# A graph network on one core: source parts, runs of products and window adds re-planned over the last forty units

## The reference

```python
coef = w_comp[etype]
msg = sum_b (x[src] @ weight[b]) * coef[:, b] * norm            # 8 bases
x1 = layernorm(x + relu(segment_sum(msg, dst) + bias_param))
neigh = segment_sum(x1[src] + edge_attr, dst)
h = ((1 + eps) * x1 + neigh) @ W1 + b1                          # 256 wide
out = layernorm(x1 + relu(batchnorm(h)) @ W2 + b2)
```

## Time and profile before

| | us |
|---|---|
| median of 3 runs (lowest, highest) | 617.11 (615.18, 617.66) |
| the profiled execution: its own time, its span | 616.46, 614.7 |
| PE busy, DVE busy, POOL busy, ACT busy | 504.3, 458.2, 402.5, 215.1 |

### The profile page before, as it was taken

How to read it: one execution, slowest core, us unless ns; L and a number is a source line. 1 busy time by engine, 2 the same in 40 slices (tenths; PEclk the granted TensorE clock), 3 DMA queues, 4 the chain that set the end, 5 groups by cost and what they waited for, 6 DMA issues and landing times.

```text
span 614.7 us, 12766 instructions
## 1 busy us (share of the span) xinstructions
PE 504.3 (82%) x3965; PEld 424.5 (69%) x3965; DVE 458.2 (75%) x1812; ACT 215.1 (35%) x309; POOL 402.5 (65%) x434
## 2 busy tenths in 40 slices
PE   4669787887887967887968899788989898799894
PEld 3448676676776655875657787677879897678574
DVE  6998999989887687985798788977753655335466
ACT  9904445453433342432433433333300000002373
POOL 6777777777777777777777777777777777500000
PEclk9988999997887997987997999889989999889998
DMA  5423757574655673755766768664665864650003
GB/s 133 121 54 98 264 184 225 171 241 147 215 172 159 206 237 105 249 158 187 226 216 189 250 213 281 218 222 136 241 209 176 275 217 129 215 192 2 2 11 96
DMA packets 98712, 108.18 MB, mean 176 GB/s; under 512 B 10949, under 2 KB 85686, under 8 KB 98642
## 3 DMA queue, kind: packets, MB, share of 16 engines
q1 hardware_dynamic: 79650, 77.81, 38.4%
q0 software_dynamic: 13312, 27.29, 16.0%
q10 hardware_dynamic: 5680, 2.23, 1.4%
HBM read 81.73 MB, written 25.56 MB: 175 GB/s over the span
## 4 chain that ended last, share of the span: by engine, by line
PE 45%; DVE 34%; DMA 10%; issue 5%; DVEq 2%; POOL 2%; ACT 1%; SPq 0%; ACTq 0%; POOLq 0%
PE psum L1190 15%; PE psum L1107 8%; DVE etype_hot L1573 7%; PE psum L1165 7%; DMA gathered_flat<-in_x_dram,src_i 6%; PE psum L1098 6%; DVE etype_hot L1570 5%; DVE sums_flat L1685 5%; PE psum L1131 4%; DVE weighted L1460 3%; DMA sums_flat<-in_x_dram 3%; POOL gathered_flat L808 2%; DVE adj_flat L1432 2%; PE psum L1328 1%; DVE sums_flat L1650 1%
## 5 line engine op out<-in xcount | busy, mean ns | idle before, releaser
L808 POOL DMA_INDIRECT gathered_flat<-in_x_dram,src_i x416 | 400.2, 962 | 129.8 <-issue 87.5
L893 ACT ACTIVATE adj_flat<-psum 128x500 f16<-128x500 f32 (+1 forms) x208 | 127.3, 612 | 245.4 <-PE psum L1131 239.4
L1098 PE MATMUL psum<-hot,attrs 128*128 128x60 f32 (+3 forms) x832 | 155.9, 274 | 2.4 <-DVE weighted L1460 2.4
L1107 PE MATMUL psum<-weighted,gathered_flat 128*128 128x96 f32 (+1 forms) x832 | 138.3, 292 | 20.1 <-DMA gathered_flat<-in_x_dram,src_i 20.0
L1098 PEld LDWEIGHTS psum<-hot,attrs 128*128 128x128 f32 x832 | 144.2, 207 | 11.7 <-issue 9.2
L1685 DVE TENSOR_TENSOR sums_flat<-psum,sums_flat 128x180 f32 x208 | 71.5, 344 | 101.8 <-PE psum L1098 72.1
L1107 PEld LDWEIGHTS psum<-weighted,gathered_flat 128*128 128x128 f32 x832 | 121.3, 205 | 23.2 <-DMA gathered_flat<-in_x_dram,src_i 23.1
L1573 DVE TENSOR_SCALAR etype_hot<-iota_key,key_t 128x300 f16<-128x300 f16 (+1 forms) x416 | 137.1, 332 | 0.0
L1131 PE MATMUL psum<-etype_hot 128*128 128x300 f16 (+1 forms) x416 | 126.9, 330 | 6.4 <-DVE etype_hot L1573 6.3
L1570 DVE TENSOR_SCALAR etype_hot<-iota_key,gathered_flat 128x128 f16<-128x128 f16 x416 | 107.0, 257 | 0.0
L1190 PE MATMUL psum<-sums_flat 128*128 128x264 f16 x594 | 76.5, 286 | 10.8 <-DVE weighted L1460 10.8
(11 more groups left out here) (154 smaller groups left out, 351.1 us busy)
## 6 DMA issues: line engine op xcount, KB each, us to landing
attrs<-in_edge_attr_dram SPq DMA_DIRECT2D x51, 512.0 KB
adjacency<-adj_flat SPq DMA_DIRECT2D x26, 900.0 KB, 6.2
gathered_flat<-in_x_dram,src_i POOLq DMA_INDIRECT x416, 3.6
coef<-adjacency SPq DMA_DIRECT2D x23, 288.0 KB, 5.5
sums_flat<-adjacency SPq DMA_DIRECT2D x9, 576.0 KB, 6.0
sums_flat<-adjacency SPq DMA_DIRECT2D x13, 288.0 KB, 5.5
sums_flat<-adjacency SPq DMA_DIRECT2D x6, 432.0 KB, 5.5
out_dram<-gathered_flat SPq DMA_DIRECT2D x5, 256.0 KB
```

The costliest lines, as they stand in the source:

```text
L808: pool.indirect_dma_start(gathered[:, t % (RING * GROUP), :], None, x[:, :], bass.IndirectOffsetOnAxis(src_i[:, t:t + 1], 0)).then_inc(gat ...
L893: nc.scalar.activation(window, counts, ACT.Copy).then_inc(counts_copied, 1)
L1098: product = nc.tensor.matmul(echoed_row(u, i), attrs[:, s * GROUP + j, :], hot_tiles(s, i)[:, u % GU, :].unsqueeze(1) .to_broadcast([P, EC ...
L1107: nc.tensor.matmul(unit_psum(u)[:, 0:B, STARTS[i]:STARTS[i] + WIDTHS[i]], gathered[:, (u * UNIT + i) % (RING * GROUP), 0:F], weighted_tile ...
```

## The change

- A looped part of one tile (tile 22) is added; the rest, tiles 23 and 24, become one late part of 181 columns in place of 256 and 53. Its 16-bit parts are kept in the buffer of the attributes, which ACT zeroes past the 53 rows (`zero_late_rows`). DVE's `zero_rest_parts` goes.
- Parts that are finished after counting has ended ("tight": the last three) start at once and have their steps closer together.
- After couple 83 a run may follow every unit, in bank 7, 4, 3 or 5 by `u % 4`, so that bank 7's runs stand after the first unit of a group. `LAST_RUN_UNIT` is 203. From couple 84 the plan has 32 runs with 130 tiles; before it had 20 with 108.
- From couple 86 DVE adds the windows of the last couple's runs ahead of the sums of its own.
- Seven blocks are opened by fills (tiles 20 to 22), which a later step closes in the same bank: two fills after units 206 and 207, five while the late part is normalised, then the first 16-bit part of tiles 23 and 24 for all seven (`first_parts`), then the thirteen finals. What is left to fills and finals: 51 tiles, 73 before.
- SP loads four of the blocks for fills and finals two groups before the end, and the other nine once the last gather has landed; before, seven were issued together during the last group. DVE reads all window places of the finals in couples 98 to 102.

```diff
-    PART_TILES = (4, 4, 4, 4, 2, 2, 2)
+    PART_TILES = (4, 4, 4, 4, 2, 2, 2, 1)
...
-    PARTS += ((LATE_AT, CHUNKS * CHUNK - LATE_AT), (CHUNKS * CHUNK, REST))
-    LATE = (LOOPED, LOOPED + 1)
-    assert max(PART_TILES) == CT and all(n % 2 == 0 for n in PART_TILES) and 0 < N - LATE_AT <= 512
+    LATE_TILES = HIGHS - PART_AT[LOOPED]
+    PARTS += ((LATE_AT, N - LATE_AT),)
+    assert max(PART_TILES) == CT and 0 < N - LATE_AT <= 512 and LATE_TILES == 2
     PART_OF = [(k, h - first // P) for h in range(HIGHS) for k, (first, n) in enumerate(PARTS)
...
-    BACK_AT, ROOT_AT, TURN_AT, KEEP_AT = 1, 3, 8, 9
-    RESIDUAL, NORM, SPLIT, OWN = 0, 2, 3, 5
+    ALL_COUNTED = min(w for w in range(COUPLES) if counted(2 * w) == U)
+    TIGHT = [done_unit(k) > 2 * ALL_COUNTED for k in range(LOOPED)]
+    FIRST = [-(-(done_unit(k) + (0 if TIGHT[k] else 2)) // 2) * 2 for k in range(LOOPED)]
+    AGG_AT = [FIRST[k] + (PART_TILES[k] + 1) // 2 * 2 for k in range(LOOPED)]
+    BACK_AT, ROOT_AT = 1, 3
+    TURN_AT = [5 if TIGHT[k] else 8 for k in range(LOOPED)]
+    KEEP_AT = [TURN_AT[k] + 1 for k in range(LOOPED)]
+    RESIDUAL = 0
+    NORM, SPLIT, OWN = ([tight if TIGHT[k] else wide for k in range(LOOPED)] for tight, wide in ((1, 2), (1, 3), (3, 5)))
...
+    def lead(w):
+        return 2 if w > ALL_COUNTED else 3
...
-    def run_bank_of(w):
+    def run_bank_of(u):
+        w = u // 2
+        if w > ALL_COUNTED:
+            return (7, 4, 3, 5)[u % 4]
+        if u % 2 == 0:
+            return None
         if w % 2 == 0:
             return 7
-        if w > ALL_COUNTED:
-            return 3
-        held = any(first - 2 <= 2 * w + 1 <= at + KEEP_AT + 1 for first, at in zip(FIRST, AGG_AT))
+        held = any(first - 2 <= u <= at + keep + 1 for first, at, keep in zip(FIRST, AGG_AT, KEEP_AT))
...
-            ready = sum(2 * w >= at + 2 * SPLIT + 3 for at in AGG_AT)
+        for u in range(LAST_RUN_UNIT + 1):
+            w = u // 2
+            if run_bank_of(u) is None:
+                continue
+            ready = sum(u >= AGG_AT[k] + 2 * SPLIT[k] + (3 if TIGHT[k] else 4) for k in range(LOOPED))
...
-                if 2 * step + 2 + LEAD <= w:
-                    runs.append((w, b, reached[b], reached[b] + parts, place, step))
+                if 2 * step + 2 + lead(w) <= w:
+                    runs.append((u, b, reached[b], reached[b] + parts, place, step))
...
-    TAIL = spaced(FILLED_BLOCKS, [])
-    LOAD_ORDER = TAIL + [b for b in range(BLOCKS) if b not in TAIL]
-    TAIL = spaced(LOAD_ORDER, TAIL)
-    FINALS = [(b, LAST_RUNS[b][1], PART_AT[LOOPED]) for b in TAIL[:FILL_COUNT]]
-    FINALS += [(b, PART_AT[LOOPED] if b in FILLED_BLOCKS else LAST_RUNS[b][1], HIGHS) for b in TAIL[FILL_COUNT:]]
-    assert all(first < last for _, first, last in FINALS) and len(FINALS) == FILL_COUNT + BLOCKS
-    FINAL_BANKS = (7, 3, 4, 6, 5, 1)
+    TAIL = spaced(BY_REST[FILL_COUNT:], spaced(BY_REST[0:FILL_COUNT], []))
+    FILLS = [(b, LAST_RUNS[b][1]) for b in TAIL[0:FILL_COUNT]]
+    LOAD_ORDER = TAIL
+    assert all(first < PART_AT[LOOPED] for _, first in FILLS)
+    FINAL_BANKS = (7, 4, 6, 5, 1, 3, 2, 0)
+    EARLY_LOADS = 4
...
-                    if g == GROUPS - 1:
-                        load_late_rows_of_x()
-                        for b in LOAD_ORDER[0:6] + LOAD_ORDER[12:13]:
+                    if g == GROUPS - 2:
+                        for b in LOAD_ORDER[0:EARLY_LOADS]:
                             load_last(b)
-                for b in LOAD_ORDER[6:12]:
+                load_late_rows_of_x()
+                sp.wait_ge(gather_in[(U - 1) % RU], U // RU * 16 * UNIT)
+                for b in LOAD_ORDER[EARLY_LOADS:]:
                     load_last(b)
...
+            def zero_late_rows():
+
+                act.wait_ge(sums_mm, COUPLES - GU // 2)
+                n = LATE_TILES * P
+                for r, used in ((0, PARTS[LOOPED][1]), (1, (LATE_TILES - 1) * P)):
+                    zeros = nc.scalar.activation(attrs_flat[:, r * n + used:(r + 1) * n],
+                                                 zero_col[:, 0:1].to_broadcast([P, n - used]), ACT.Copy)
+                zeros.then_inc(rest_zeroed, 1)
...
+                def fill_products(n):
+                    b, first = FILLS[n]
+                    pe.wait_ge(last_in[n], 16)
+                    pe.wait_ge(parts_ready, LOOPED)
+                    block_products(wait_for_bank(n), tiles_in(last_buffer(b), first, first, PART_AT[LOOPED]), closes=False)
...
-                    if u % 2 and u // 2 in RUN_AT:
-                        run_products(RUN_AT[u // 2])
+                    if u in RUN_AT:
+                        run_products(RUN_AT[u])
+                    if u >= U - 2:
+                        fill_products(u - (U - 2))
...
+                    b = TAIL[n]
+                    at = LAST_RUNS[b][1]
+                    first = PART_AT[LOOPED] if n < FILL_COUNT else at
+                    if n >= FILL_COUNT:
+                        pe.wait_ge(last_in[n], 16)
+                        bank = wait_for_bank(n)
                     else:
-                        earlier = [m for m in range(NRUNS) if run_bank(m) == bank]
-                        if earlier:
-                            pe.wait_ge(nbr_added, BLOCK * (earlier[-1] + 1))
-                        if bank == 6:
-                            pe.wait_ge(x1_kept, LOOPED)
-                        if bank < 6:
-                            pe.wait_ge(counts_copied, U)
-                    block_products(bank, tiles)
+                        bank = FINAL_BANKS[n]
+                    pe.wait_ge(parts_ready, LOOPED + 1)
+                    block_products(bank, tiles_in(last_buffer(b), at, first, HIGHS), opens=n >= FILL_COUNT,
+                                   parts=(0, 1, 2) if n >= FILL_COUNT else (1, 2))
+
+                def first_parts(n):
+                    b = TAIL[n]
+                    pe.wait_ge(parts_step, 3 * LOOPED + 1)
+                    block_products(FINAL_BANKS[n], tiles_in(last_buffer(b), LAST_RUNS[b][1], PART_AT[LOOPED], HIGHS),
+                                   opens=False, closes=False, parts=(0,))
...
+                turn_back(LOOPED)
+                for n in range(2, FILL_COUNT):
+                    fill_products(n)
+                turn_norm(LOOPED)
                 for n in range(FILL_COUNT):
-                    final_products(n)
-                for k in LATE:
-                    turn_norm(k)
-                for n in range(FILL_COUNT, len(FINALS)):
+                    first_parts(n)
+                for n in range(BLOCKS):
                     final_products(n)
...
-                    if w - 1 in RUN_AT:
-                        firsts = block_bases(RUNS[RUN_AT[w - 1]][1])
+                    if COUPLES - 6 <= w < COUPLES - 1:
+                        b = len(last_bases) // BLOCK
+                        last_bases += block_bases(b, min(3, BLOCKS - b))
+                    runs = [n for n in range(NRUNS) if RUNS[n][0] // 2 == w - 1]
+                    firsts = {n: block_bases(RUNS[n][1]) for n in runs}
+                    for k in range(LOOPED):
+                        if w == AGG_AT[k] // 2 + OWN[k] + 1:
+                            dve.wait_ge(own_added, k + 1)
+                    adds = [(n, j) for n in runs for j in range(BLOCK)]
+                    if w > ALL_COUNTED + 2:
+                        if adds:
+                            dve.wait_ge(added, 2 * w)
+                        for n, j in adds:
+                            add_run(n, j, firsts[n])
+                        adds = []
                     dve.wait_ge(sums_mm, w + 1)
-                    if runs_before(w - 1) > runs_before(w - 2):
-                        dve.wait_ge(nbr_added, BLOCK * runs_before(w - 1))
-                    for k in range(LOOPED):
-                        if w == AGG_AT[k] // 2 + OWN + 1:
-                            dve.wait_ge(own_added, k + 1)
+                    finished = runs_before(w if w > ALL_COUNTED + 2 else w - 1)
+                    if finished:
+                        dve.wait_ge(nbr_added, BLOCK * finished)
...
+                chunk_residual(LOOPED)
+                chunk_norm(LOOPED)
+                chunk_split(LOOPED, 0)
+                chunk_split(LOOPED, 1)
+                dve.wait_ge(nbr_added, BLOCK * NRUNS)
+                chunk_own(LOOPED)
+                dve.wait_ge(own_added, LOOPED + 1)
```

270 lines of the change are left out of this document (121 added, 149 removed).

## The result

On the first chip the changed kernel takes 638.09 us (median of 4 runs, 637.43 to 639.44), the kernel before 617.38 (4 runs, 615.18 to 617.9). The ratio is 1.0355 (95% interval 1.0329 to 1.038), so 20.7 us slower. I had predicted 621.5 (610 to 628): slower is right, the size is not.

The account below looks back on a forecast made before the run. The prediction took PE's waits for DVE, not gathers, as what counts. Waits of 18.2 us plus 4.8 of slow clock made 23.0 against 18.0 before, 5 us slower: 616.46 becomes 621.5, range 610 to 628.

Parts of the forecast that it names:

- units 168, 172, 176 and 180: PE's runs in bank 7 wait there for DVE's select: 3.3, 1.15, 1.3 and 3.4 us.
- 184, 188 and 200: Shorter PE waits for DVE at these units: 0.36 us each at 184 and 188, 0.6 at 200.
- One of the signs: Sign that the forecast is right: PE leaves unit 207 at 553 to 562 us.
- units 197 and 205: PE's wait in `turn_norm` right behind DVE's normalising: 0.4 and 0 to 2.4 us, entered as 0.4 and 0.6.
- unit 198: The one-tile part's bases wait for DVE's sums of unit 197: 4.0 us without loads, 4.6 with.
- after 207: `bases` waits for DVE's last sums, with DVE ending 1.8 to 3.2 us behind PE: entered as 2.1.
- so I expose one or so at each place where DVE is late: About one uncovered register load, 0.52 us on DVE's queue, of two to four at the heads of couples 86 to 102.
- the three long waits: Slow clock behind PE's long waits: 1.6 us of loss, seen after one of 2.27 us, charged as 4.8 in all.
- the collision: SP's loads slow the last gathers; its end is worth 3.0 us only to a PE waiting for gathers, so nothing.
- late loads: The nine loads of counts behind the last gather have over 10 us, so they cost nothing.
- ring and POOL: PE may fall 40 us behind the gathers before POOL stops; it falls 25 behind, so no cost.
- everything exposed: Rival: all register loads uncovered, 22 us of waits and 6.4 of clock, ending at 627 or more; chance 0.08.

Follow-up runs that it names:

- c0: The changed kernel with no edit, on a slower chip: 757.7 us, ratio 1.0043 to the kernel before.
- c1: The changed kernel with the base numbers of the last 13 blocks read in the tail again: 758.5 us, ratio 1.0074 to the kernel before.
- g8: The changed kernel with runs behind odd units alone from unit 168 on (49 runs, not 63): 747.4 us, ratio 0.993 to the kernel before.
- g0: The changed kernel with no edit, on another slower chip than c0: 758.6 us, ratio 1.0078 to the kernel before.
- e8: The same kernel as g8 (runs behind odd units alone), on another slower chip: 753.5 us, ratio 0.9869 to the kernel before.
- b0: The kernel before, unedited, with a trace on a slower chip: 763.2 us, one run.
- g9: g8 plus the 13 blocks' base numbers read in couples 64 to 72 and late runs' base numbers one couple earlier: 746.5 us, ratio 0.9914 to the kernel before.
- e5: The changed kernel with the 13 blocks' base numbers read in couples 64 to 72, ahead of the unit sums: 763.3 us, ratio 1.0012 to the kernel before.

## Why the prediction was wrong in size

**Right.** The direction, and the work: 975 products in both. PE waits 3.17, 1.20, 1.33 and 3.88 us at units 168, 172, 176 and 180 (predicted 3.3, 1.15, 1.3, 3.4); twice 0.44 and 0.74 for 184, 188 and 200 (0.7 and 0.6 together); no wait for gathers; 40.5 us of dense layers. From the bases at 576.00 to the last product at 595.1 it is 19.1 us (tail 18.9), with a wait of 0.5 ahead of it and not 2.1. One of the signs was missed: unit 207 was left at 574.5, not at 553 to 562.

**First failed step: units 197 and 205, "0.4 and 0 to 2.4", entered as 0.4 and 0.6.** They were 2.06 + 1.19 and 4.10, 7.35 in place of 1.0. In part this was given back at unit 198 (3.26 for 4.6) and after 207. The reason is the sentence "so I expose one or so at each place where DVE is late": ahead of unit 205 there stand, from 556.6 on, two groups of three reads, one of three blocks and two of one in each, 2.5 us a group. In the trace nothing covers them: DVE stands idle for 2.58 us ahead of the window add at 565.59, while PE waits for it. The reads of three blocks I had not priced apart at all. Without them the waits for the normalising fell from 6.4 us (c0) to 3.4 (c1); the rest went only with fewer runs (g8). A read of one block was priced right (0.52 us, measured 0.51), so the error lay in the cover and in the long reads. The Trainium skill gives about 200 ns for each register that a `TENSOR_LOAD` reads, also in bulk (Runtime: NRT & Kernel Launch, section "Instruction fetch mechanics"). The trace agrees for these reads, whose values lie apart in the buffer: 1.40 less 0.51 is 0.22 us for each of the four further registers. It does not agree for the four values of a group's own read (line 1699), which lie side by side: they take 0.35 us together (minimum, median and longest of a read in ns, then when):

```profile
L1699 DVEq TENSOR_LOAD <-base_row x52: 339/349/1567, 48.3 to 569.8; - x52
L1675 DVEq TENSOR_LOAD <-base_row x68: 507/519/2495, 154.0 to 571.3; - x68
```

Both medians are also under the floor of some 600 ns that the prediction cites from the Trainium skill (DMA: Bandwidth & Descriptors, section "Latency and other measured facts"); the measurement decides. I had also not seen that the run behind `turn_norm` at 197 waits for a split that DVE does behind the normalising (1.19). Idle time came to 22.9 where I had 18.2.

**Second failed step: the clock, "I charge that to the three long waits, 4.8".** It cost about 11 us. The wait that I took for the price was one of 2.27 us, followed by 1.6 us of loss. Behind 3.17 us that held (3.2 us at 1.2 GHz, 2.96 of them busy, so 1.5 lost); behind the others it was more: 6.6 us at 1.2 GHz behind 3.88, 10.1 behind 2.06, 1.19 and 3.26, 6.7 behind 4.10. The kernel before held a dearer case than the one I took, which I had read only as an average (0.82):

```profile
536.40:543.20 6.80, 6.37 (x30) 4.98 (x30) 1.28 (x4) 0.00 (x0) 0.00 (x0) 0.50 0.56 207
```

It stands behind a stop of 1.89 us and cost about 3. In c0, g0, e8 and b0 too, slow stretches follow most stops of 1.8 us or more (12 of 14, the other two lie in a stretch that was slow already) and few of the shorter ones. But stops do not explain all: in g9, whose longest stop is 1.6 us, PE was at 1.2 GHz for 18 of the 136 us. Over the stretch, 22.9 us of idle time came with about 11 of slow clock. This is read from traces; no run changed the clock alone, and what sets it is not shown.

**Third: the 5.1 us before unit 168,** which the prediction took to be equal. 1.7 are slow clock behind the stop of 1.94 us at 444.16: from the start of these 24 products to the next unit it is 4.37 us. In the kernel before it is 2.70, and the same stop there is 1.48 us long, so another 0.5 is the longer stop. The other 3.0 were there at unit 164, where both plans issue the same on PE. On chip D the kernels reach unit 168 at 568.1 and 567.1. Why it was 5 on the first chip stays open.

The three together, 4.7 of idle time, 6.2 of clock and 5.1, are 16.0; the profiled execution took 637.43, 15.9 above my number.

**The costs put at nothing:** the collision, late loads, ring and POOL cost nothing (no wait for a gather or a load stands among PE's waits, and POOL idles 130.1 us, before 129.8). The early reads' cover, which I did not ask for, was what failed. The rival *everything exposed* (627, "or more where a wait that I did not see joins", chance 0.08) was nearest. That its 22 us of waits come so close to 22.9 is luck: it exposed loads at other places, and units 198 and the end came in 2.9 below my own terms. Its clock, 6.4, was too low too.

**How far it is shown.** That DVE's late work makes the stops is shown by runs on the other chips, where the same stops stand in the same places and shrink or go with the edits. How much each edit would take off the 20.7 us of the first chip is not shown.

## What to carry to other kernels

Moving TensorE work forward pays only as long as the engine that must fold its results in can follow. Here 12 more late runs brought 24 more window adds and 12 more register reads to a VectorE for which PE already waited 6.6 us. Two ways out gave about 1% each against the kernel before: fewer late runs, although 36 products went back to the tail, or all runs with the reads moved ahead, each with the run that waits for the select one unit later. Ask of each read what it waits behind, and take its price from a read of the same length and layout. A read hoisted from one busy place to another gained nothing in time (c1 against c0); read where VectorE waited for PE, it cost nothing in the stretch or in the tail (e5).

## What the runs showed of the hardware

- A register read on DVE took 0.51 us for two registers and 1.40 for six, whose values lie apart in the buffer, and 0.35 for four that lie side by side.
- On four other chips the kernel before took 22 to 23% longer. POOL started a gather every 1.57 us in b0 (399.3 and 253.5 us over 416) and every 1.27 on the first chip, and DVE and PE paused too with nothing shown that they waited for. My expectations say that the engines stood still together; I saw that in one place of one trace only, and there PE's products went on. Over the 44 pauses of POOL of over 2 us in b0, PE was busy for about half of the time, so that wording was wrong. The cause is not known. The two kernels differ by 3.6% on the first chip and by 0.4 to 0.8% there: a change that adds waits looks better on a chip that stalls.
- In the changed kernel's trace the clock fell to 1.2 GHz behind stops of 1.9 us and more, and stayed there for 3.3 to 10.1 us; in c0 one such stretch was 13.7. It also fell where no stop was so long: in the kernel before at 522.7 us, behind one of 1.1, and in g9.
